# Row softmax in a graph layer: one exponential of 1024 columns in every step in place of one of 2048 in every second

## The chip, the cores and the metric

The kernel runs on one core of one Trainium2 chip. The metric is the device time of one execution in microseconds (us). A core has TensorE (PE, matrix products; weight loads are listed apart as PEld), VectorE (DVE), ScalarE (ACT), GpSimd (POOL) and SyncE (SP), each with its own instruction stream; they meet only through semaphores.

## The reference

4096 rows `x` attend to 4096 neighbours under a 0/1 matrix `adj`:

```python
h = relu(layernorm(x))
neib_att = tanh(neigh @ Wn1 + bn1) @ Wn2 + bn2        # 4096 x 32
value    = neigh @ Wv + bv                            # 4096 x 128
x_att    = tanh(h @ Wx1 + bx1) @ Wx2 + bx2            # 4096 x 32
ws = leaky_relu(x_att @ neib_att.T, 0.01)             # 4096 x 4096
ws = softmax(where(adj > 0, ws, NEG_BIG), axis=1)
out = x + concatenate([h @ Wfx + bfx, ws @ value], axis=1)
```

All inputs and the output are float32, `adj` is int32. The softmax is over all 4096 neighbours of a row.

## The kernel before, in words

**Tiles.** A tile is 128 rows of `x` by all 4096 neighbours; it is cut into 4 chunks of 1024 columns (`CHUNK`, `CHUNKS`). One chunk is a step `s`; 32 tiles make 128 steps. Four tiles make a round of 16 steps (`GSTEPS`), for which new rows of `x` are normalised, turned and projected as side work. Two tiles make a group `g` of 8 steps, whose weights are multiplied with `value` together.

**A chunk's way.** In step `s`:
- VectorE makes the bf16 mask of `adj` (`mask_of`, L679), two steps ahead.
- TensorE makes scores in the PSUM tile `ps` (`score`, L913 and L914). `ps` has two buffers, so the scores of step `s` wait on `leaked` of step `s - 2`. From step 11 on the mask of the upper 512 columns is not added here.
- ScalarE stores `Relu(99 * ps)` in `scores` (`rise`, L551).
- GpSimd adds the mask to the upper half of that (L455).
- VectorE, one step later, computes `(ps + scores) * 0.01`, which is the leaky relu, stores it in `scores`, and keeps the running maximum of the row in `top` (`leak`, L708). The reduction over a chunk starts from the entry of the chunk before, so the four leaks of a tile form a chain. After the fourth, `negate` (L719) writes `neg_top`, the bias of the exponential.
- ScalarE, five steps after the scores (`EXP_LAG`), takes the exponential in place with its row sums (`power`, L563). It does so for two chunks at once, in every second step: exponentials of 128 x 2048 in odd steps, none in even ones. An exponential with row sums is two records in the trace, an ACTIVATE and an ACTIVATION_READ_ACCUMULATOR.
- TensorE, eleven steps after the scores (`BACK_LAG`), turns 128 x 128 blocks of the exponentials into the PSUM tile `pt` (`turn`, L936), in two turns a step. Each turn is split into two float32r parts: `pt_hi` by ScalarE (`hi`, L525), `pt_lo` by VectorE (`lo`, L690). TensorE multiplies both with `value` in three products (`product`, L957 to L959), two turns behind. A turn waits on the `pt_lo` of two turns before, because `pt` has two buffers.
- When a group is through, ScalarE copies the product to `agg` (`aggregate`, L533), TensorE turns it back (L968), and VectorE scales it with the reciprocal of the row sums and adds it to `x` (L764).

**Order.** There is no scheduler. Each engine's stream is written out by its function `step(s)`:

```python
# ScalarE                         # VectorE                        # TensorE
hi(s, 0)                          leak(s)      # chunk s - 1       score(s, 0); score(s, 1)
aggregate(s)                      lo(s, 0)                         turn(s, 0)
rise(s)                           negate(s)                        product(s, -2)
hi(s, 1)                          close(s); neigh_rest(s)          turn(s, 1)
side(s)                           x_work(s)                        side(s)
power(s)                          lo(s, 1)                         product(s, -1)
                                  mask_of(s + 2)                   agg_turn(s)
```

Of the kernel before, what the change touches and what calls it, by code (L numbers as in the profile page):

```python
# [25 lines left out]
FP32 = mybir.dt.float32  # L26
# [3 lines left out]
ALU = mybir.AluOpType  # L30
ACT = mybir.ActivationFunctionType
AX = mybir.AxisListType

P = 128
# [7 lines left out]
CHUNK = 2 * BANK  # L42
CHUNKS = N_NEIGH // CHUNK
STEPS = GROUPS * TILES * CHUNKS
# [10 lines left out]
SLOPE = 0.01  # L55
# [10 lines left out]
TURN_X = 4  # L66
FILL = (6, 6, 6, 4, 0, 0, 0, 0)
EXP_LAG = CHUNKS + 1
HALF = 2 * CHUNK
HALVES = N_NEIGH // HALF  # L70
BACK_LAG = ASTEPS + 3
COPY_LAG = BACK_LAG + ASTEPS + 1
# [28 lines left out]
def build(nc, x, adj, neigh_t, small_of, wide_of, value_of, out):  # L101
    with ExitStack() as ctx:
        def sb(name, shape, dt):
            return ctx.enter_context(nc.sbuf_tensor(name, shape, dt))

        def sem(name):
            return ctx.enter_context(nc.semaphore(name))
# [16 lines left out]
        wide_x = sb("wide_x", [P, WIDE], FP32)  # L124
        ident = sb("ident", [P, P], FP32)
        ident_bf16 = ident.bitcast(BF16)[:, 1:2 * P:2]
        top = sb("top", [P, 2, CHUNKS], FP32)
        neg_top = sb("neg_top", [P, 2, 1], FP32)
        sums = sb("sums", [P, 2, TILES, HALVES], FP32)
        row_sum = sb("row_sum", [P, AT], FP32)  # L130
        inv_sum = sb("inv_sum", [P, 2, AT], FP32)
# [37 lines left out]
        ps = ctx.enter_context(nc.psum_tensor("ps_scores", [P, 2, CHUNK], FP32))  # L169
# [34 lines left out]
        risen = sem("risen")  # L204
        masked = sem("masked")
        leaked = sem("leaked")
        top_done = sem("top_done")
        exp_done = sem("exp_done")
        block_turned = sem("block_turned")
        hi_done, lo_done = sem("hi_done"), sem("lo_done")  # L210
# [66 lines left out]
        def chunk_of(s):  # L277

            return s // GSTEPS % 2, s // CHUNKS % TILES, s % CHUNKS
# [187 lines left out]
        def _(act):  # L467
# [85 lines left out]

            def power(s):
                e = s - EXP_LAG
                if 0 <= e < STEPS and e % 2 == 0:
                    parity, tile, c = chunk_of(e)
                    if c == 0:
                        act.wait_ge(top_done, e // CHUNKS + 1)
                        if tile == 0 and e >= 2 * GSTEPS:  # L560
                            act.wait_ge(sums_done, (e // GSTEPS - 1) * TILES // AT)
                    cols = scores[:, parity * TILES + tile, c * CHUNK:c * CHUNK + HALF]
                    act.activation(cols, cols, ACT.Exp, bias=neg_top[:, tile % 2, :],  # L563
                                   accum_out=sums[:, parity, tile, c // 2:c // 2 + 1]).then_inc(exp_done, 1)

            def side(s):
                if s == 0:
# [11 lines left out]
            def step(s):  # L579
                hi(s, 0)  # L580
                aggregate(s)
                rise(s)
                hi(s, 1)
                side(s)
                power(s)
# [5 lines left out]
        def _(dve):  # L591
# [74 lines left out]
            def mask_of(n):  # L666

                k = n
                if ADJ_RING <= n < ADJ_RING + FRONT:
                    source = adj_front[:, n - ADJ_RING, :]  # L670
                    dve.wait_ge(front_ready[(n - ADJ_RING) // LOAD], 16)
                else:
                    source = adj_in[:, n % ADJ_RING, :]
                    dve.wait_ge(adj_ready[n % ADJ_RING // LOAD], 16 * ((n - FRONT if n >= ADJ_RING else n) // ADJ_RING + 1))
                if n >= MASK_RING:
                    dve.wait_ge(scored, n - MASK_RING + 1)
                if n - MASK_RING >= POOL_MASKS:
                    dve.wait_ge(masked, n - MASK_RING + 1 - POOL_MASKS)
                dve.tensor_scalar(mask[:, n % MASK_RING, :], source, 0.0, MASKED, ALU.is_le,  # L679
                                  ALU.mult).then_inc(mask_done, 1)  # L680

            def lo(s, u):
                b = s - BACK_LAG
                if not 0 <= b < STEPS:
                    return
                j = 2 * b + u
                dve.wait_ge(hi_done, j + 1)
                if 2 * b + u >= 2:
                    dve.wait_ge(block_used, j - 1)
                dve.tensor_tensor(pt_lo[:, u], pt[:, u], pt_hi[:, (2 * b + u) % HI_RING].bitcast(FP32),  # L690
                                  ALU.subtract).then_inc(lo_done, 1)

            def leak(s):
                n = s - 1
                if not 0 <= n < STEPS:
                    return
                parity, tile, c = chunk_of(n)
                cols = scores[:, parity * TILES + tile, c * CHUNK:(c + 1) * CHUNK]
                dve.wait_ge(risen, n + 1)
                if n >= POOL_MASKS:  # L700
                    dve.wait_ge(masked, n + 1 - POOL_MASKS)
                if c:
                    dve.wait_ge(leaked, n)
                start = top[:, tile % 2, c - 1:c] if c else -3.0e38
                if c == 0 and n >= 2 * CHUNKS:
                    dve.wait_ge(top_done, n // CHUNKS - 1)
                dve.sem_inc(joined, 1)
                dve.tensor_tensor_reduce(cols, ps[:, n % 2], cols, SLOPE, start, ALU.add, ALU.max,  # L708
                                         top[:, tile % 2, c:c + 1]).then_inc(leaked, 1)

            def negate(s):
                n = s - 1
                if not 0 <= n < STEPS or n % CHUNKS != CHUNKS - 1:
                    return
                dve.wait_ge(leaked, n + 1)
                if n >= 2 * CHUNKS:

                    dve.wait_ge(exp_done, (n // CHUNKS - 1) * HALVES)
                dve.tensor_scalar(neg_top[:, n // CHUNKS % 2, :], top[:, n // CHUNKS % 2, CHUNKS - 1:CHUNKS],  # L719
                                  -1.0, None, ALU.mult).then_inc(top_done, 1)  # L720

            def neigh_rest(s):
                if value_due(s - 2) is not None:
                    value_low(value_due(s - 2))
                if s == 1:
                    att_low(1, NEIGH_GROUPS - 1)

            def x_work(s):
                if s == AHEAD_STATS:
                    for i in range(TILES):  # L730
                        x_stats(1, i)
                    x_aggr(1)
                for i in range(TILES):
                    if (e := x_due(s, X_STATS[i])) > 1:
                        x_stats(e, i)
                if (e := x_due(s, X_AGGR)) > 1:
                    x_aggr(e)
                if e := x_due(s, X_STACK[1]):
                    x_stack_low(e, e % 2, x_bank_late(e))
                if s == LEFT_0:  # L740
                    x_left_out(0, pa[:, 0, :])
                if e := x_due(s, X_LEFT):
                    x_left_out(e, x_bank_late(e))

            def close(s):
                b = s - SUM_LAG
                if b >= 0 and b % ASTEPS == 0 and b // ASTEPS < AGROUPS:
                    g = b // ASTEPS
                    first = g % (TILES // AT) * AT
                    dve.wait_ge(exp_done, (g + 1) * AT * HALVES)  # L750
                    wait(dve, sums_done, g)
                    dve.reduce_sum(row_sum[:, :], sums[:, g // (TILES // AT) % 2, first:first + AT],
                                   axis=AX.X).then_inc(row_sum_done, 1)
                    dve.wait_ge(row_sum_done, g + 1)
                    wait(dve, right_done, g - 1)
                    dve.reciprocal(inv_sum[:, g % 2, :], row_sum[:, :]).then_inc(sums_done, 1)
                b = s - FIN_LAG
                if b >= 0 and b % ASTEPS < AT and b // ASTEPS < AGROUPS:
                    g, i = b // ASTEPS, b % ASTEPS
                    if i == 0:  # L760
                        dve.wait_ge(agg_turned, g + 1)
                        dve.wait_ge(sums_done, g + 1)
                        dve.wait_ge(right_summed, g + 1)
                    last = dve.scalar_tensor_tensor(  # L764
                        right_of(g)[:, i, :], product_of(g)[:, i * P:(i + 1) * P], inv_sum[:, g % 2, i:i + 1],
                        right_of(g)[:, i, :], ALU.mult, ALU.add)
                    if i == AT - 1:
                        last.then_inc(right_done, 1)

            def step(s):  # L770
                if s < POOL_MASKS:
                    mask_of(s + 2)
                leak(s)
                lo(s, 0)
                negate(s)
                close(s)
                neigh_rest(s)
                x_work(s)
                lo(s, 1)
                if POOL_MASKS <= s < STEPS - 2:  # L780
                    mask_of(s + 2)
# [261 lines left out]
```

## Time and profile before

| | us |
|---|---|
| median of 3 runs | 489.14 (488.77 to 489.36) |
| the profiled execution | 488.76 |
| its span in the trace | 486.8 |
| TensorE busy | 467.1 |
| VectorE busy | 426.0 |
| ScalarE busy | 410.8 |
| GpSimd busy | 258.5 |

The first 31 us are the preparation of the neighbours, steps 0 to 10 fill the pipeline, steps 11 to 127 run all stages beside each other, and from 453 us on only turns and products are left. A group of instructions is shown by line, engine, operation, output and inputs. The busy time of TensorE holds overlapping pipelined products, so a high share says that it is the engine to watch, not that no time is lost on it; the waits say more. A step's place is found by counting: the n-th Relu of L551 is step n, the n-th pair of L525 copies is step 11 + n.

### The profile page before, as it was taken

What the parts mean: (1) busy time and instruction counts of PE and PEld (TensorE: products, weight loads), DVE (VectorE), ACT (ScalarE), POOL (GpSimd) and SP (SyncE); (2) the same over time, 40 slices, a digit from 0 to 9 for tenths busy, and PEclk for the clock granted to TensorE, in tenths of its full rate; (3) what the DMA queues carried; (4) which work ended last, traced back from release to release, by engine and by line L of the source; (5) the groups of instructions that cost most, each with busy time, mean ns of one, the idle gap of its engine ahead of it and who ended that gap; (6) DMA issues with size and microseconds to landing.
All of it is one profiled execution on the core that took longest, in us unless ns stands there. A gap on an engine that the chain in (4) does not pass through costs nothing.

```text
span 486.8 us, 10746 instructions
## 1 busy us (share of the span) xinstructions
PE 467.1 (96%) x3728; PEld 423.8 (87%) x3728; DVE 426.0 (88%) x852; ACT 410.8 (84%) x586; POOL 258.5 (53%) x361
## 2 busy tenths in 40 slices
PE   7987889999999999999999999999999999999897
PEld 7975679998899989998998989998999989988896
DVE  4678999989989999999999998989999888989654
ACT  2455898899988999899898998899889998999763
POOL 3108147844686457745685458745694555453200
PEclk9999999999999999999999999999999999999999
DMA  8944635557456754566445854476546465551000
GB/s 316 284 91 88 151 66 88 99 93 158 86 88 110 143 104 83 107 123 136 82 95 87 173 100 73 93 140 120 104 78 130 82 110 85 102 95 37 10 12 13
DMA packets 32373, 51.51 MB, mean 106 GB/s; under 512 B 2368, under 2 KB 22976, under 8 KB 32320
## 3 DMA queue, kind: packets, MB, share of 16 engines
q0 software_dynamic: 9216, 33.56, 42.1%
q1 hardware_dynamic: 22816, 17.17, 11.0%
q8 instruction: 30, 0.49, 0.4%
q10 hardware_dynamic: 288, 0.10, 0.1%
q14 instruction: 23, 0.19, 0.1%
HBM read 80.19 MB, written 4.19 MB: 173 GB/s over the span
## 4 chain that ended last, share of the span: by engine, by line
PE 74%; ACT 5%; issue 4%; DVE 4%; POOL 2%; DVEq 0%; ACTq 0%; POOLq 0%
PE ps_turned L936 20%; PE ps_product L957 11%; PE ps_product L959 11%; PE ps_product L958 11%; PE ps_scores L914 10%; PE ps_scores L913 6%; PE ps_product L879 3%; POOL scores L455 2%; ACT scores L551 2%; DVE pt_lo L690 2%; ACT scores L563 1%; PE ps_product L855 1%; ACT pt_hi L525 1%; PE ps_product L871 1%; DVE mask L679 1%
## 5 line engine op out<-in xcount | busy, mean ns | idle before, releaser
L690 DVE TENSOR_TENSOR pt_lo<-ps_turned,pt_hi 128x512 fp32r<-128x512 f32 x256 | 173.5, 686 | 35.3 <-ACT pt_hi L525 23.9
L455 POOL TENSOR_TENSOR scores<-scores,mask 128x512 f32<-128x512 f32 x117 | 136.2, 1164 | 118.6 <-ACT scores L551 118.4
L525 ACT ACTIVATE pt_hi<-ps_turned 128x512 fp32r<-128x512 f32 x256 | 155.4, 607 | 42.6 <-PE ps_turned L936 41.6
L957 PE MATMUL ps_product<-pt_hi,v_hi 128*128 128x256 f32 x512 | 165.0, 322 | 0.1
L936 PE MATMUL ps_turned<-ident,scores 128*128 128x128 f32 x1024 | 154.5, 273 | 2.0 <-DVE pt_lo L690 1.7
L959 PE MATMUL ps_product<-pt_lo,v_hi 128*128 128x256 f32 x512 | 144.3, 282 | 0.0
L958 PE MATMUL ps_product<-pt_hi,v_lo 128*128 128x256 f32 x512 | 144.0, 281 | 0.0
L551 ACT ACTIVATE scores<-ps_scores 128x1024 f32<-128x1024 f32 x128 | 132.1, 1032 | 10.3 <-PE ps_scores L914 10.3
L936 PEld LDWEIGHTS ps_turned<-ident,scores 128*128 128x128 f32 x1024 | 121.2, 140 | 21.6 <-DVE pt_lo L690 3.9
L563 ACT ACTIVATE scores<-scores,neg_top 128x2048 f32<-128x2048 f32 x64 | 129.1, 2018 | 0.0
L708 DVE CUSTOM_DVE_ANT_0 scores<-ps_scores,scores,top 128x1024 f32<-128x1024 f32 x96 | 122.5, 1276 | 1.1 <-ACT scores L551 0.9
L914 PE MATMUL ps_scores<-neib,xs 128*128 128x512 f32 x256 | 106.7, 496 | 0.0
L957 PEld LDWEIGHTS ps_product<-pt_hi,v_hi 128*128 128x128 f32 x512 | 97.3, 190 | 1.5 <-issue 1.2
L958 PEld LDWEIGHTS ps_product<-pt_hi,v_lo 128*128 128x128 f32 x512 | 97.3, 190 | 0.0
L959 PEld LDWEIGHTS ps_product<-pt_lo,v_hi 128*128 128x128 f32 x512 | 96.3, 188 | 0.0
L913 PE MATMUL ps_scores<-mask,ident 128*128 128x512 bf16 x139 | 53.6, 386 | 10.3 <-DVE top L708 6.3
L418 POOL DMA_DIRECT2D adj_in<-in_adj x60 | 35.4, 589 | 39.7 <-DVE mask L679 36.7
L679 DVE TENSOR_SCALAR mask<-adj_in 128x1024 bf16<-128x1024 bf16 x120 | 56.1, 469 | 0.1
L914 PEld LDWEIGHTS ps_scores<-neib,xs 128*128 128x128 f32 x256 | 49.5, 193 | 3.2
L708 DVE CUSTOM_DVE_ANT_0 scores<-ps_scores,scores 128x1024 f32<-128x1024 f32 x32 | 38.9, 1216 | 1.0 <-ACT scores L551 1.0
L913 PEld LDWEIGHTS ps_scores<-mask,ident 128*128 128x128 bf16 x139 | 13.4, 97 | 22.4 <-issue 17.3
L404 POOL TENSOR_SCALAR x_rows<-x_rows,mean_var,rstd 128x256 f32<-128x256 f32 x24 | 30.1, 1256 | 0.0
(71 smaller groups left out, 349.4 us busy)
## 6 DMA issues: line engine op xcount, KB each, us to landing
adj_in<-in_adj POOLq DMA_DIRECT2D x60, 512.0 KB, 5.5
scores<-in_neigh_t SPq DMA_DIRECT2D x8, 512.0 KB, 7.7
x_rows<-in_x SPq DMA_DIRECT2D x7, 512.0 KB, 5.7
x_left<-in_x SPq DMA_DIRECT2D x8, 256.0 KB, 5.7
x_right<-in_x SPq DMA_DIRECT2D x16, 128.0 KB, 5.2
scores<-in_adj POOLq DMA_DIRECT2D x4, 512.0 KB, 6.6
out_h<-x_left SPq DMA_DIRECT2D x8, 256.0 KB, 2.4
out_h<-x_right SPq DMA_DIRECT2D x16, 128.0 KB, 2.4
```

Of the source, the lines that this page charges most:

```text
L455: pool.tensor_tensor(half, half, mask[:, s % MASK_RING, BANK:CHUNK], ALU.add).then_inc(masked, 1)
L525: act.activation(pt_hi[:, (2 * b + u) % HI_RING], pt[:, u], ACT.Copy).then_inc(hi_done, 1)
L551: act.activation(scores[:, parity * TILES + tile, c * CHUNK:(c + 1) * CHUNK], ps[:, s % 2], ACT.Relu, scale=RISE).then_inc(risen, 1)
L563: act.activation(cols, cols, ACT.Exp, bias=neg_top[:, tile % 2, :], accum_out=sums[:, parity, tile, c // 2:c // 2 + 1]).then_inc(exp_done, 1)
L690: dve.tensor_tensor(pt_lo[:, u], pt[:, u], pt_hi[:, (2 * b + u) % HI_RING].bitcast(FP32), ALU.subtract).then_inc(lo_done, 1)
L708: dve.tensor_tensor_reduce(cols, ps[:, n % 2], cols, SLOPE, start, ALU.add, ALU.max, top[:, tile % 2, c:c + 1]).then_inc(leaked, 1)
L913: pe.matmul(ps[:, s % 2, half], ident_bf16, mask[:, s % MASK_RING, half], start=True, stop=False)
L914: last = pe.matmul(ps[:, s % 2, half], xs[:, parity, tile * P:(tile + 1) * P], neib[:, c * CHUNK + h * BANK:c * CHUNK + (h + 1) * BANK], s ...
L936: last = pe.transpose(pt[:, u, (k * AT + i) * P:(k * AT + i + 1) * P], scores[:, (g * AT + i) % (2 * TILES), (n * SPAN + k) * P:(n * SPAN ...
L957: pe.matmul(product_of(g), v_hi[:, block, :], high, start=block == 0, stop=False)
L958: pe.matmul(product_of(g), v_lo[:, block, :], high, start=False, stop=False)
L959: last = pe.matmul(product_of(g), v_hi[:, block, :], low, start=False, stop=block == BLOCKS - 1)
```

## The change

The exponential handles one chunk (`HALF = CHUNK`), in every step, with one entry of row sums for each chunk. The scores are stored negated (slope -0.01), with the running minimum in `low_top`; the exponential has scale -1 and takes the last entry of `low_top` as its bias directly. `negate`, `neg_top` and the semaphore `top_done` are gone. The exponential of a tile's first chunk waits on `leaked` instead. The leak of a tile's first chunk, which overwrites an entry pair of `low_top`, waits on `exp_done` of all chunks of two tiles before.

```diff
-HALF = 2 * CHUNK
+HALF = CHUNK
@@ ScalarE
             def power(s):
                 e = s - EXP_LAG
-                if 0 <= e < STEPS and e % 2 == 0:
+                if 0 <= e < STEPS:
                     parity, tile, c = chunk_of(e)
                     if c == 0:
-                        act.wait_ge(top_done, e // CHUNKS + 1)
+                        act.wait_ge(leaked, (e // CHUNKS + 1) * CHUNKS)
                         if tile == 0 and e >= 2 * GSTEPS:
                             act.wait_ge(sums_done, (e // GSTEPS - 1) * TILES // AT)
                     cols = scores[:, parity * TILES + tile, c * CHUNK:c * CHUNK + HALF]
-                    act.activation(cols, cols, ACT.Exp, bias=neg_top[:, tile % 2, :],
-                                   accum_out=sums[:, parity, tile, c // 2:c // 2 + 1]).then_inc(exp_done, 1)
+                    act.activation(cols, cols, ACT.Exp, bias=low_top[:, tile % 2, CHUNKS - 1:CHUNKS], scale=-1.0,
+                                   accum_out=sums[:, parity, tile, c:c + 1]).then_inc(exp_done, 1)
@@ VectorE
-                start = top[:, tile % 2, c - 1:c] if c else -3.0e38
+                start = low_top[:, tile % 2, c - 1:c] if c else 3.0e38
                 if c == 0 and n >= 2 * CHUNKS:
-                    dve.wait_ge(top_done, n // CHUNKS - 1)
+                    dve.wait_ge(exp_done, (n // CHUNKS - 1) * HALVES)
                 dve.sem_inc(joined, 1)
-                dve.tensor_tensor_reduce(cols, ps[:, n % 2], cols, SLOPE, start, ALU.add, ALU.max,
-                                         top[:, tile % 2, c:c + 1]).then_inc(leaked, 1)
-
-            def negate(s):
...
+                dve.tensor_tensor_reduce(cols, ps[:, n % 2], cols, -SLOPE, start, ALU.add, ALU.min,
+                                         low_top[:, tile % 2, c:c + 1]).then_inc(leaked, 1)
@@ VectorE, step(s)
                 leak(s)
                 lo(s, 0)
-                negate(s)
                 close(s)
```

The order on ScalarE before, in steps 23 to 25 (a round's steps 7 to 9), from the second copy of step 23; L563 is the exponential, L525 the `pt_hi` copy, L551 the Relu, L502 a copy of side work:

```order
L525 ACTIVATE pt_hi<-ps_turned 128x512 [waits block_used,block_turned]
L563 ACTIVATE scores,sums<-scores,neg_top 128x2048 [waits top_done]
L525 ACTIVATE pt_hi<-ps_turned 128x512 [waits block_used,block_turned]
L551 ACTIVATE scores<-ps_scores 128x1024 [waits scored]
L525 ACTIVATE pt_hi<-ps_turned 128x512 [waits block_used,block_turned]
L502 ACTIVATE x_rows_t<-ps_product 128x512 [waits x_wide,x_turned]
L525 ACTIVATE pt_hi<-ps_turned 128x512 [waits block_used,block_turned]
L551 ACTIVATE scores<-ps_scores 128x1024 [waits scored]
L525 ACTIVATE pt_hi<-ps_turned 128x512 [waits block_used,block_turned]
L563 ACTIVATE scores,sums<-scores,neg_top 128x2048
```

The same place of ScalarE in the changed kernel, where L561 is the exponential, L523 the `pt_hi` copy, L549 the Relu and L500 the copy of side work:

```order
L523 ACTIVATE pt_hi<-ps_turned 128x512 [waits block_used,block_turned]
L561 ACTIVATE scores,sums<-scores,low_top 128x1024 [waits leaked]
L523 ACTIVATE pt_hi<-ps_turned 128x512 [waits block_used,block_turned]
L549 ACTIVATE scores<-ps_scores 128x1024 [waits scored]
L523 ACTIVATE pt_hi<-ps_turned 128x512 [waits block_used,block_turned]
L500 ACTIVATE x_rows_t<-ps_product 128x512 [waits x_wide,x_turned]
L561 ACTIVATE scores,sums<-scores,low_top 128x1024
L523 ACTIVATE pt_hi<-ps_turned 128x512 [waits block_used,block_turned]
L549 ACTIVATE scores<-ps_scores 128x1024 [waits scored]
L523 ACTIVATE pt_hi<-ps_turned 128x512 [waits block_used,block_turned]
L561 ACTIVATE scores,sums<-scores,low_top 128x1024
```

Between two Relus of this stretch there is now exactly one exponential, where every second gap had none.

The order on VectorE before, around the first leak of a tile (the second L708 pair; the first is the fourth leak of the tile before), L690 being `pt_lo`:

```order
L708 ISA scores,top<-ps_scores,scores,top 128x1024 [waits leaked,risen,masked]
L708 ISA top 128x1
L690 TENSOR_TENSOR pt_lo<-ps_turned,pt_hi 128x512 [waits block_used,hi_done]
L719 TENSOR_SCALAR neg_top<-top 128x1 [waits exp_done,leaked]
L690 TENSOR_TENSOR pt_lo<-ps_turned,pt_hi 128x512 [waits block_used,hi_done]
L679 TENSOR_SCALAR mask<-adj_in 128x1024 [waits masked,scored,adj_ready1]
L708 ISA scores,top<-ps_scores,scores 128x1024 [waits top_done,risen,masked]
```

And in the changed kernel:

```order
L706 ISA scores,low_top<-ps_scores,scores,low_top 128x1024 [waits leaked,risen,masked]
L706 ISA low_top 128x1
L688 TENSOR_TENSOR pt_lo<-ps_turned,pt_hi 128x512 [waits block_used,hi_done] x2
L677 TENSOR_SCALAR mask<-adj_in 128x1024 [waits masked,scored,adj_ready1]
L706 ISA scores,low_top<-ps_scores,scores 128x1024 [waits exp_done,risen,masked]
```

The instruction between the two `pt_lo` is gone, and the wait on `exp_done` has moved from it to the first leak of the next tile. The orders of TensorE, GpSimd and SyncE hold the same instructions as before.

## Rows read from the trace of the kernel before

**Rows 1.** The page's busy times: us, share of the span, instructions.

```profile
PE 467.1 (96%) x3728; PEld 423.8 (87%) x3728; DVE 426.0 (88%) x852; ACT 410.8 (84%) x586; POOL 258.5 (53%) x361
```

**Rows 2.** Busy time of each engine in steps 64 to 79, then clock, DMA.

```profile
239.00:293.07 54.07, 53.60 (x422) 49.11 (x420) 50.61 (x103) 49.32 (x71) 34.32 (x47) 1.00 0.59 108
```

**Rows 3.** Waits, 77.37 to 401.16 us: who for whom: total, times, longest.

```profile
PEld ps_scores L913 <- issue: 5.2, 16, 0.4
...
PE ps_scores L913 <- DVE top L708: 2.0, 10, 0.2
PEld ps_turned L936 <- DVE pt_lo L690: 1.5, 6, 0.3
...
PEld ps_product L968 <- ACT agg L533: 1.1, 6, 0.2
```

**Rows 4.** Waits, 401.16 to 453 us.

```profile
PEld ps_scores L913 <- issue: 0.9, 2, 0.4
```

**Rows 5.** TensorE in order of time, steps 72 to 74: start, us, instruction.

```profile
266.18 0.60 PE L936 MATMUL ps_turned<-ident,scores 128*128 128x128 f32 x4
...
268.93 0.39 PE L913 MATMUL ps_scores<-mask,ident 128*128 128x512 bf16 x1
...
269.62 0.60 PE L936 MATMUL ps_turned<-ident,scores 128*128 128x128 f32 x4
...
271.93 0.39 PE L913 MATMUL ps_scores<-mask,ident 128*128 128x512 bf16 x1
```

**Rows 6.** ScalarE in order of time, steps 71 to 73.

```profile
265.53 2.02 ACT L563 ACTIVATE scores<-scores,neg_top 128x2048 f32<-128x2048 f32 x1
267.43 0.21 ACT L563 ACTIVATION_READ_ACCUMULATOR scores<-scores,neg_top 128x1 f32 x1
267.51 0.60 ACT L525 ACTIVATE pt_hi<-ps_turned 128x512 fp32r<-128x512 f32 x1
267.99 1.04 ACT L551 ACTIVATE scores<-ps_scores 128x1024 f32<-128x1024 f32 x1
268.90 0.62 ACT L525 ACTIVATE pt_hi<-ps_turned 128x512 fp32r<-128x512 f32 x1
269.37 0.64 ACT L502 ACTIVATE x_rows_t<-ps_product 128x512 f32<-128x512 f32 x1
270.26 0.60 ACT L525 ACTIVATE pt_hi<-ps_turned 128x512 fp32r<-128x512 f32 x1 [0.25 <-PE ps_turned L936]
```

**Rows 7.** VectorE in order of time: leaks of steps 72 and 73, `pt_lo` before.

```profile
269.55 0.69 DVE L690 TENSOR_TENSOR pt_lo<-ps_turned,pt_hi 128x512 fp32r<-128x512 f32 x1 [0.65 <-ACT pt_hi L525]
...
270.49 1.22 DVE L708 CUSTOM_DVE_ANT_0 scores<-ps_scores,scores 128x1024 f32<-128x1024 f32 x1
...
273.23 1.28 DVE L708 CUSTOM_DVE_ANT_0 scores<-ps_scores,scores,top 128x1024 f32<-128x1024 f32 x1
```

**Rows 8.** ScalarE's groups by shape: busy us, mean ns, idle before.

```profile
L525 ACT ACTIVATE pt_hi<-ps_turned 128x512 fp32r<-128x512 f32 x256 | 155.4, 607 | 42.6 <-PE ps_turned L936 41.6
L551 ACT ACTIVATE scores<-ps_scores 128x1024 f32<-128x1024 f32 x128 | 132.1, 1032 | 10.3 <-PE ps_scores L914 10.3
L563 ACT ACTIVATE scores<-scores,neg_top 128x2048 f32<-128x2048 f32 x64 | 129.1, 2018 | 0.0
L563 ACT ACTIVATION_READ_ACCUMULATOR scores<-scores,neg_top 128x1 f32 x64 | 13.2, 207 | 0.0
...
L506 ACT ACTIVATE agg<-ps_product,small_x 128x128 f32<-128x128 f32 x8 | 3.2, 402 | 0.0
```

**Rows 9.** The tail in order of time, steps 131 and 132.

```profile
461.43 0.63 PE L936 MATMUL ps_turned<-ident,scores 128*128 128x128 f32 x4 [0.96 <-DVE pt_lo L690]
...
463.74 2.00 ACT L563 ACTIVATE scores<-scores,neg_top 128x2048 f32<-128x2048 f32 x1
```

**Rows 10.** ScalarE in order of time, steps 9 and 10.

```profile
58.57 2.04 ACT L563 ACTIVATE scores<-scores,neg_top 128x2048 f32<-128x2048 f32 x1
...
60.55 1.06 ACT L551 ACTIVATE scores<-ps_scores 128x1024 f32<-128x1024 f32 x1
```

More of the change, by code:

```diff
@@ L126, in build @@
         ident_bf16 = ident.bitcast(BF16)[:, 1:2 * P:2]
-        top = sb("top", [P, 2, CHUNKS], FP32)
-        neg_top = sb("neg_top", [P, 2, 1], FP32)
+        low_top = sb("low_top", [P, 2, CHUNKS], FP32)
         sums = sb("sums", [P, 2, TILES, HALVES], FP32)
@@ L206, in build @@
         leaked = sem("leaked")
-        top_done = sem("top_done")
         exp_done = sem("exp_done")
@@ L703, in leak @@
                     dve.wait_ge(leaked, n)
-                start = top[:, tile % 2, c - 1:c] if c else -3.0e38
+                start = low_top[:, tile % 2, c - 1:c] if c else 3.0e38
                 if c == 0 and n >= 2 * CHUNKS:
-                    dve.wait_ge(top_done, n // CHUNKS - 1)
+                    dve.wait_ge(exp_done, (n // CHUNKS - 1) * HALVES)
                 dve.sem_inc(joined, 1)
-                dve.tensor_tensor_reduce(cols, ps[:, n % 2], cols, SLOPE, start, ALU.add, ALU.max,
-                                         top[:, tile % 2, c:c + 1]).then_inc(leaked, 1)
-            def negate(s):
[L712 to L720, printed above, removed]
+                dve.tensor_tensor_reduce(cols, ps[:, n % 2], cols, -SLOPE, start, ALU.add, ALU.min,
+                                         low_top[:, tile % 2, c:c + 1]).then_inc(leaked, 1)
             def neigh_rest(s):
```

## Prediction

> **What bounds the kernel now.** I read the busy shares first: TensorE 467.1 of 486.8 us, VectorE 426.0, ScalarE 410.8 [rows 1]. Three engines lie within 14%, so a share alone does not name the bound. The granted clock is 1.00 in the busy row of a full 16-step round, 239.00 to 293.07 us; there TensorE is busy 53.60 of 54.07 us, VectorE 50.61, ScalarE 49.32 [rows 2]. So the clock plays no part, TensorE is nearly the bound, and what can be won is the small idle time that is left on it.
>
> The waits say what that idle time is. From step 16 (77.37) to step 112 (401.16) TensorE waits 5.2 + 2.0 us before a step's score products, 1.5 us before a turn for the low halves `pt_lo`, and 1.1 us for the `agg` copy: 9.8 us in six rounds [rows 3]. In the sixteen steps after that it is 0.9 us before scores [rows 4]. The wait before scores is for `leaked` of two steps ago, since `ps` has two buffers.
>
> The reason stands in the order of time. Steps 72 and 73 of TensorE start their turns at 266.18 and 269.62 [rows 5]. ScalarE runs a 2048-column exponential in the odd step 71 (265.53, readout 267.43), and only then comes to the first `pt_hi` copy of step 72 at 267.51, which is 1.33 us after the turn started. In step 73 no exponential precedes, and the copy starts at 270.26, 0.64 us after its turn, having waited 0.25 us for TensorE [rows 6]. Every later hand-over inherits this: the Relu of step 72 starts at 267.99 (1.81 after the turn), then comes GpSimd's mask addition, and VectorE's leak of step 72 starts at 270.49, or 4.31 us after the turn of that step. For step 73 the leak comes at 273.23, 3.61 after the turn [rows 7]. The even steps are thus about 0.7 us late, and it is their leak that releases the scores two steps later.
>
> **What the change removes.** The 32 `negate` instructions go from VectorE: 426.0 us is not its bound, each lies in a place where VectorE waits 0.65 us for ScalarE's next `pt_hi` [rows 7], so I count them at nothing. Negative scale and slope, and the minimum for the maximum, use the same two instructions on tiles of the same size: nothing, with no row that says otherwise. If the leak were dearer by 0.1 us in the negated form, VectorE would still have 1.6 us less work than a round lasts (50.61 + 1.6 against 54.07), so it would be covered.
>
> **What it adds: 64 exponentials and 64 readouts.** ScalarE has 512 columns in 607 ns and 1024 in 1032 ns, so 0.83 ns per column and a fixed 0.18 us; a 128-column tanh with a bias tile takes 402 ns, so about 0.30 us fixed. The exponential of 2048 takes 2018, of which 1.70 are columns: 0.32 us fixed [rows 8]. One of 1024 should take 0.85 + 0.32 = 1.17 us. In order of time an instruction hands over before its end: 1.90 us from exponential to readout, 0.08 from readout to the next copy [rows 6]. So one of 1024 occupies 1.17 - 0.12 + 0.08 = 1.13 us, two occupy 2.26 where one of 2048 occupied 1.98. That is +0.28 us a pair, 17.9 us of ScalarE time in the kernel. The bounds: below, half of the old one each (0.99, no cost at all); above, the full 1.17 plus the full 207 ns of a readout (1.37, +0.76 a pair). I take 1.13, since it is made of the nearest rows.
>
> Is there room? A round gets 8 extra pairs' cost, 8 x 0.28 = 2.2 us: ScalarE goes from 49.32 to 51.6 of 54.07 [rows 2]. It fits, and stays below TensorE's 53.60. Without side work a ScalarE step becomes 0.48 + 0.90 + 0.48 + 1.13 = 2.99 us (the first three from the starts in [rows 6]), and TensorE's step without side work lasts 3.00 (268.93 to 271.93 [rows 5]). The engines match within a row's accuracy: a copy that starts 0.64 after its turn starts so again a step later. ScalarE loses ground only in steps with side work of its own, about 0.3 to 0.5 us, and TensorE nearly always has side work in the same or the next steps.
>
> The Trainium skill, "ScalarE: Activation LUTs", section "What ACT_TABLE_LOAD costs", speaks against the change: an ACTIVATE whose bias is a per-partition operand costs some 280 ns beside its columns whatever its size, and neighbours overlap by some 93 ns, so cutting one in two buys nothing and costs a fixed part. For the old exponential it gives 1986 ns, and the trace agrees with 2018 [rows 8]. By it the addition would be an estimated 12 us of ScalarE for the 64 more, without a price for the readouts, against my 17.9; if ScalarE were the bound, either would be lost time.
>
> **What it moves.** ScalarE now meets an exponential in every step, after the step's second copy, where before it met two steps' worth in odd steps. The copy of even steps should begin 0.64 instead of 1.33 after its turn, and Relu, mask addition and leak move forward with it, from 4.31 to about 3.61. That leak ends near 3.61 + 1.22 = 4.83 after the turn of its step; the scores that need it follow at least 2 x 3.00 - 0.69 = 5.31 after (0.69: 268.93 to 269.62 [rows 5]). TensorE then does not wait for it. The last chunk of a row is exponentiated one step later than before; its block turns come three and more steps after that, and so I count nothing.
>
> **The new wait.** The leak of each row's first chunk now waits until ScalarE has finished the exponentials of two rows before, the last of which stands at the end of the step before. On time, ScalarE reaches its end at 0.64 + 1.86 + 1.13 = 3.63 after the turn, with the semaphore about 3.7. The leak itself would start at 3.61: 0.1 us later in each of 30 rows, within the 0.48 us of slack just found (5.31 against 4.83). Where ScalarE has a `x_rows_t` copy ahead of that exponential (step 8 of a round) it is some 0.5 later still; the transposes put 0.44 us more on TensorE there too (step 72 lasts 3.44 [rows 5]). So 0.1 us each over 7 rounds, 0.7 us in all. Behind this leak on VectorE stand both `pt_lo` of the step and the next mask; their readers are a step later on TensorE, with over half a microsecond in hand.
>
> **The sum.** Of the 9.8 us in the six rounds I take two thirds, 6.5; the rest belongs to GpSimd's normalisation, to side work and to places that have no exponential ahead of them. The 0.9 us in steps 112 to 127 I take whole, since less side work stands there. In the tail, TensorE stands 0.96 us at 461.43 behind an exponential, and the one at 463.74 (2.00 us) delays copies and `agg` again [rows 9]: 1.5 together, since a 1.13 us exponential fits a 2.3 us tail step. In the opening the exponential at 58.57 holds the Relu of step 10 until 60.55 [rows 10]; one that occupies 1.13 us in place of 1.98 gives 0.85, say 0.9. Together 6.5 + 0.9 + 1.5 + 0.9 = 9.8, less 0.7 for the new wait and 1.0 for lateness through ScalarE's side work: 8.1 us. The profiled execution took 488.76 us, so 480.7. The median of the runs is 489.14, 0.4 more, of which I add a small part: 480.8 us.
>
> **Rivals.**
> A, most of the gain is not there (TensorE's idle time has other causes, or the next thing is late by as much: `pt_lo`, the mask, GpSimd). For it speaks that only 0.47 us of a 54.07 us round is idle on TensorE [rows 2]; against it, that the busy time contains short waits between pipelined products, and the waits listed are 1.6 us a round. Then a quarter to a third of 9.8 remains: about 486.
> B, nothing measurable: gain and new wait cancel, 488.8. It needs 0.3 us at each of the 30 first chunks.
> C, slower: ScalarE becomes the bound. Place: every step, through the fixed part of the exponential and its readout. At 1.37 us each a round has 49.32 + 8 x 0.76 = 55.4 us of ScalarE work, 1.3 more than it lasts now; over 7 rounds +9, less 2.4 kept in opening and tail: 495. It decides from an occupancy at which 16 exponentials cost 54.07 - 49.32 = 4.75 us more than 8 old ones: (8 x 1.98 + 4.75) / 16 = 1.29 us each. Against it stand the overlaps seen in [rows 6]. The late first leak would add to it, since both come from the same lateness.
> D, the change does not even the steps out: ScalarE's order would have to keep two exponentials together. The order has one in each step, so I give this no chance of its own.
>
> **How the numbers follow.** Forecast 0.60, within 477.5 to 484: the low end takes the waits whole (9.8 + 0.9 + 1.5 + 0.9, less 1.7, is 11.4), the high end half of them (6.5 less 1.7 is 4.8). A 0.18, B 0.08, C 0.14. What can be told from no change here is 0.2%, about 1 us. Faster has the forecast and A, and a little of B: 0.79; same 0.08; slower 0.13. The range reaches from 477 to 489.5, through A and B; most of C is left out.
>
> **What would show it.** The exponential of 1024 near 1.17 us and its occupancy near 1.13. The first copy of even and of odd steps both 0.6 to 0.9 us after the turn. A round of 52.9 to 53.4 us instead of 54.07. Waits before scores reduced to a third, while ScalarE is busy some 428 us (410.8 + 17.9). VectorE waiting at first chunks for ScalarE's exponential, 0.1 us at a time, would confirm the new wait; waits of 0.3 us and more there, passed on to TensorE's scores, would make the prediction wrong, as would ScalarE without idle time in a round.

## The result, and the profile after

| | us |
|---|---|
| before, median (4 runs) | 489.25 (488.77 to 489.43) |
| changed, median (4 runs) | 485.37 (484.90 to 485.68) |
| ratio | 0.9929, interval 0.9917 to 0.9941 |
| changed, the profiled execution | 485.15, span 482.8 |

The change makes the kernel 3.9 us faster, where 8.3 were forecast: the direction was right and the time lies inside the range, but the gain is under half of the forecast.

The page's busy times, beside [rows 1]:

```profile
PE 464.3 (96%) x3728; PEld 424.5 (88%) x3728; DVE 427.7 (89%) x820; ACT 428.3 (89%) x714; POOL 258.4 (54%) x361
```

ScalarE has 17.5 us more, as forecast (17.9). VectorE lost 32 instructions (4.6 us in the group of L719) and is busy 1.7 us longer all the same; that is the first hint of something that the prediction did not contain. It is the masks that grew, with their number and shape unchanged; the group in the kernel before, then in the changed one:

```profile
L679 DVE TENSOR_SCALAR mask<-adj_in 128x1024 bf16<-128x1024 bf16 x120 | 56.1, 469 | 0.1
```

```profile
L677 DVE TENSOR_SCALAR mask<-adj_in 128x1024 bf16<-128x1024 bf16 x120 | 61.1, 510 | 0.1
```

The groups of ScalarE, beside [rows 8]:

```profile
L561 ACT ACTIVATE scores<-scores,low_top 128x1024 f32<-128x1024 f32 x128 | 151.5, 1183 | 0.0
...
L561 ACT ACTIVATION_READ_ACCUMULATOR scores<-scores,low_top 128x1 f32 x128 | 29.5, 230 | 0.0
```

The same steps 71 to 73 of ScalarE in order of time (start, us, instruction), beside [rows 6]:

```profile
265.38 1.22 ACT L561 ACTIVATE scores<-scores,low_top 128x1024 f32<-128x1024 f32 x1
266.43 0.27 ACT L561 ACTIVATION_READ_ACCUMULATOR scores<-scores,low_top 128x1 f32 x1
266.52 0.66 ACT L523 ACTIVATE pt_hi<-ps_turned 128x512 fp32r<-128x512 f32 x1
266.99 1.10 ACT L549 ACTIVATE scores<-ps_scores 128x1024 f32<-128x1024 f32 x1
...
268.85 1.26 ACT L561 ACTIVATE scores<-scores,low_top 128x1024 f32<-128x1024 f32 x1
269.89 0.30 ACT L561 ACTIVATION_READ_ACCUMULATOR scores<-scores,low_top 128x1 f32 x1
269.98 0.70 ACT L523 ACTIVATE pt_hi<-ps_turned 128x512 fp32r<-128x512 f32 x1
```

TensorE's first turns of steps 72 and 73:

```profile
265.84 0.60 PE L922 MATMUL ps_turned<-ident,scores 128*128 128x128 f32 x4
...
269.27 0.60 PE L922 MATMUL ps_turned<-ident,scores 128*128 128x128 f32 x4
```

An exponential of 1024 columns occupies 265.38 to 266.52, 1.14 us; forecast 1.13. The copies come 0.68 and 0.71 us after their turns, where before it was 1.33 and 0.64. For ScalarE the steps are evened out. But the round of steps 64 to 79 shrank only from 54.07 [rows 2] to 53.82 us:

```profile
238.82:292.64 53.82, 53.20 (x422) 49.07 (x420) 51.04 (x99) 51.53 (x87) 33.92 (x47) 1.00 0.58 109
```

The columns are the length, then PE, PEld, DVE, ACT, POOL, clock, DMA. ScalarE rose to 51.53 (51.6 forecast), VectorE to 51.04 from 50.61. The waits from step 16 to 112 (77.85 to 399.68), beside [rows 3]:

```profile
PEld ps_scores L899 <- issue: 5.9, 18, 0.5
DVE scores L706 <- ACT scores L561: 5.6, 12, 0.6
...
PE ps_scores L899 <- DVE low_top L706: 1.7, 6, 0.3
...
PEld ps_turned L922 <- issue: 0.5, 3, 0.2
```

The wait for `agg` is gone, and TensorE's waits before turns fell from 1.5 us (for `pt_lo`) to 0.5, for which the trace names no cause; that is about the 2.0 us by which these six rounds became shorter (323.79 to 321.83). The waits before scores are 7.6 us where they were 7.2. They have moved to other steps. The second row is new: VectorE's leak waits for an exponential, the wait that the change added.

The opening, VectorE's leak of step 8 and then TensorE's scores of step 10:

```profile
57.97 1.23 DVE L706 CUSTOM_DVE_ANT_0 scores<-ps_scores,scores 128x1024 f32<-128x1024 f32 x1 [1.87 <-ACT scores L561]
```

```profile
59.35 0.38 PE L899 MATMUL ps_scores<-mask,ident 128*128 128x512 bf16 x1 [1.50 <-DVE low_top L706]
```

The leak of step 8, a first leak, waits 1.87 us for the exponential that ScalarE makes in step 8, and the scores of step 10 wait behind it. In the rounds the two places are the scores of a round's steps 10 and 14. VectorE, steps 73 and 77, the first leaks of two tiles, each with the mask before it:

```profile
268.84 0.69 DVE L688 TENSOR_TENSOR pt_lo<-ps_turned,pt_hi 128x512 fp32r<-128x512 f32 x1 [0.41 <-PE ps_product L945]
269.45 0.42 DVE L677 TENSOR_SCALAR mask<-adj_in 128x1024 bf16<-128x1024 bf16 x1
270.48 1.23 DVE L706 CUSTOM_DVE_ANT_0 scores<-ps_scores,scores 128x1024 f32<-128x1024 f32 x1 [0.61 <-ACT scores L561]
...
283.21 0.77 DVE L677 TENSOR_SCALAR mask<-adj_in 128x1024 bf16<-128x1024 bf16 x1
283.90 1.21 DVE L706 CUSTOM_DVE_ANT_0 scores<-ps_scores,scores 128x1024 f32<-128x1024 f32 x1
```

And GpSimd at the second place:

```profile
281.83 1.16 POOL L453 TENSOR_TENSOR scores<-scores,mask 128x512 f32<-128x512 f32 x1 [0.96 <-ACT scores L549]
282.97 0.73 POOL L363 TENSOR_TENSOR x_left<-x_left,wide_x 128x256 f32<-128x256 f32 x1
```

TensorE's last product and the scores behind it, at the first place (step 74) and at the second (step 78):

```profile
271.45 0.28 PE L945 MATMUL ps_product<-pt_lo,v_hi 128*128 128x256 f32 x1
271.86 0.38 PE L899 MATMUL ps_scores<-mask,ident 128*128 128x512 bf16 x1
...
284.68 0.28 PE L945 MATMUL ps_product<-pt_lo,v_hi 128*128 128x256 f32 x1
285.27 0.38 PE L899 MATMUL ps_scores<-mask,ident 128*128 128x512 bf16 x1 [0.31 <-DVE low_top L706]
```

The products follow each other at 0.12 us; what a start comes later than that is counted as late here. The first leak waits 0.61 us for ScalarE; the scores of step 74 then start at 271.86, 0.29 late. At the second place the leak shows no wait, but the mask ahead of it takes 0.77 us where 0.42 is its time: it starts at 283.21 while GpSimd adds to `x_left` until 283.70, and is done just under 0.3 us after that. Here the scores of step 78 are 0.47 us late. In the kernel before, the mask of this place came first and took its 0.42, and GpSimd's addition was the one that was longer, 0.91 in place of 0.73:

```profile
283.81 0.42 DVE L679 TENSOR_SCALAR mask<-adj_in 128x1024 bf16<-128x1024 bf16 x1
```

```profile
283.91 0.91 POOL L365 TENSOR_TENSOR x_left<-x_left,wide_x 128x256 f32<-128x256 f32 x1
```

The scores of this step were late in the kernel before as well. How late the scores start, by the same count, as the mean of the six rounds: a round's step 14 has 0.36 us before and 0.42 after, step 10 has 0.02 and 0.26, step 8 has 0.15 and nothing, and steps 5 and 6 together have 0.28 and 0.25. So the change took the lateness of step 8 away and added that of step 10, and in step 14 one cause took the place of another. This gave two theories beside the forecast's own: 1, the new wait; 2, the mask has moved forward into GpSimd's addition. As the third I took the longer ScalarE time itself.

### The profile page after: what moved, and what is told of

Read it like the earlier page. It is cut to its first block, busy times and chain, and to the rows that moved or that the text cites. A ratio compares the mean times of both kernels' runs of the same rounds, so it can differ in the third digit from the quotient of the medians.

```text
span 482.8 us, 10844 instructions
## 1 busy us (share of the span) xinstructions
PE 464.3 (96%) x3728; PEld 424.5 (88%) x3728; DVE 427.7 (89%) x820; ACT 428.3 (89%) x714; POOL 258.4 (54%) x361
## 4 chain that ended last, share of the span: by engine, by line
PE 75%; ACT 5%; issue 3%; DVE 3%; POOLq 0%; POOL 0%; DVEq 0%; ACTq 0%
PE ps_turned L922 20%; PE ps_product L943 11%; PE ps_product L945 11%; PE ps_product L944 11%; PE ps_scores L900 10%; PE ps_scores L899 6%; PE ps_product L865 3%; ACT scores L561 3%; ACT pt_hi L523 2%; DVE scores L706 2%; PE ps_product L857 1%; PE ps_product L841 1%; ACT scores L549 1%; PE ps_product L848 1%; PE ps_product L954 1%
## 5 line engine op out<-in xcount | busy, mean ns | idle before, releaser
L523 ACT ACTIVATE pt_hi<-ps_turned 128x512 fp32r<-128x512 f32 x256 | 158.1, 618 | 20.9 <-PE ps_turned L922 20.3
L561 ACT ACTIVATE scores<-scores,low_top 128x1024 f32<-128x1024 f32 x128 | 151.5, 1183 | 0.0
L549 ACT ACTIVATE scores<-ps_scores 128x1024 f32<-128x1024 f32 x128 | 133.3, 1041 | 9.6 <-PE ps_scores L900 9.4
L706 DVE CUSTOM_DVE_ANT_0 scores<-ps_scores,scores,low_top 128x1024 f32<-128x1024 f32 x96 | 122.5, 1276 | 0.9 <-ACT scores L549 0.4
L677 DVE TENSOR_SCALAR mask<-adj_in 128x1024 bf16<-128x1024 bf16 x120 | 61.1, 510 | 0.1
L402 POOL TENSOR_SCALAR x_rows<-x_rows,mean_var,rstd 128x256 f32<-128x256 f32 x24 | 31.6, 1319 | 0.0
```

The costliest lines, as they stand in the source:

```text
L523: act.activation(pt_hi[:, (2 * b + u) % HI_RING], pt[:, u], ACT.Copy).then_inc(hi_done, 1)
L549: act.activation(scores[:, parity * TILES + tile, c * CHUNK:(c + 1) * CHUNK], ps[:, s % 2], ACT.Relu, scale=RISE).then_inc(risen, 1)
L561: act.activation(cols, cols, ACT.Exp, bias=low_top[:, tile % 2, CHUNKS - 1:CHUNKS], scale=-1.0, accum_out=sums[:, parity, tile, c:c + 1]). ...
L706: dve.tensor_tensor_reduce(cols, ps[:, n % 2], cols, -SLOPE, start, ALU.add, ALU.min, low_top[:, tile % 2, c:c + 1]).then_inc(leaked, 1)
```

## The experiments

Each was timed in five rounds; ratios are to the kernel before on the same chip. The changed kernel's is 0.9929 [0.9917, 0.9941].

| | median us | ratio | interval |
|---|---|---|---|
| e1 wait moved to the fourth leak | 482.93 | 0.9878 | 0.9863 to 0.9893 |
| e2 split alone | 483.26 | 0.9886 | 0.9873 to 0.9900 |
| e3 negated form alone | 488.77 | 0.9998 | 0.9989 to 1.0007 |
| e4 `x_left` addition in step 14 | 483.57 | 0.9897 | 0.9884 to 0.9911 |
| e5 e1 and e4 | 481.19 | 0.9843 | 0.9829 to 0.9856 |
| e6 e5, second half in step 16 | 479.50 | 0.9807 | 0.9794 to 0.9821 |
| e7 exponentials one step earlier | 482.25 | 0.9869 | 0.9855 to 0.9882 |
| e8 e5 with two exponentials of 512 | 500.42 | 1.0238 | 1.0224 to 1.0251 |
| e9 before, addition in step 14 | 489.02 | 1.0006 | 0.9995 to 1.0016 |
| e10 before, steps 14 and 16 | 487.47 | 0.9970 | 0.9959 to 0.9981 |

**e1, the wait at the fourth leak.** Only the fourth entry of a tile's row in `low_top` is read as a bias, so only the fourth leak has to wait.

```diff
-                if c == 0 and n >= 2 * CHUNKS:
+                if c == CHUNKS - 1 and n >= 2 * CHUNKS:
                     dve.wait_ge(exp_done, (n // CHUNKS - 1) * HALVES)
```

> The changed kernel with the wait on the exponentials of two tiles before put at a tile's fourth leak in place of its first (only the fourth entry of low_top is read as a bias). Nothing else differs. Theory 1, the new wait ate the missing 4.5 us: the opening gets back 0.9 us, each of the round's stalls behind a first leak goes (0.3 to 0.5 us, 6 rounds, two a round), so 481.5 to 482.5 us against 485.4. Theory 2, the stalls come from masks that VectorE makes while GpSimd works, and the wait stands beside them: only the opening gains, 484.3 to 485. Theory 3, the longer ScalarE time as such: no difference, 485.4.

The ratio is 0.0051 lower, 2.5 us; at 482.93 us it lies 0.4 us above what theory 1 expected and below what the other two did. VectorE's first leaks of steps 8, 72 and 76, in its trace:

```profile
56.39 1.23 DVE L706 CUSTOM_DVE_ANT_0 scores<-ps_scores,scores 128x1024 f32<-128x1024 f32 x1 [0.27 <-ACT scores L549]
...
268.61 1.22 DVE L706 CUSTOM_DVE_ANT_0 scores<-ps_scores,scores 128x1024 f32<-128x1024 f32 x1
...
281.78 0.77 DVE L677 TENSOR_SCALAR mask<-adj_in 128x1024 bf16<-128x1024 bf16 x1
282.46 1.21 DVE L706 CUSTOM_DVE_ANT_0 scores<-ps_scores,scores 128x1024 f32<-128x1024 f32 x1
```

In the opening the leak comes after the Relu again (56.39 instead of 57.97), and the one of step 72 directly behind its mask. The opening up to the turn of step 16 lost 0.5 us, steps 16 to 112 lost 1.6 (321.83 to 320.21), the rest 0.2; the expectation had 0.9 for the opening. The mask before the first leak of step 76 is as long as it was. So theory 1 holds for its own places and leaves the other. Theory 3, which expected no difference, is out.

**e2 and e3, one half of the change each.** e2 keeps `top`, `neg_top` and `negate` and only splits (`neg_top` lies in an unused corner of `agg`); e3 keeps the 2048 columns and only negates.

```diff
 e2, against the kernel before
-HALF = 2 * CHUNK
+HALF = CHUNK
-                if 0 <= e < STEPS and e % 2 == 0:
+                if 0 <= e < STEPS:
-                                   accum_out=sums[:, parity, tile, c // 2:c // 2 + 1]
+                                   accum_out=sums[:, parity, tile, c:c + 1]
 e3, against the changed kernel: the same lines the other way
```

> The kernel before with exponentials of 1024 columns in every step, but the positive scores, the maximum and the negation on VectorE kept; so it has no wait of a first leak on ScalarE. Theory 1: 482 to 483 us (as e1, with the 32 negations covered). Theory 2: 484.5 to 485.5, as the changed kernel. Theory 3: the split alone gives 485.4 and the negated form nothing.

> The changed kernel with exponentials of 2048 columns in every second step: the negated form alone. The wait of a first leak is then on an exponential of an odd step before, long done. All theories: the negations were covered, so within 0.5 us of before, 488.7 to 489.5. If the negated form had a price or a gain of its own it would show here.

The whole gain is the split's. The negated form alone changes nothing that can be measured, so the 32 negations were covered, as the prediction had it. In company with the split it costs 2.1 us (0.9929 less 0.9886). In steps 16 to 112 that is the wait: e2 takes 320.24 us there, as e1 does. The opening of e2 is no such proof. Its leak of step 8 does not wait, and yet it has 46.95 us up to the turn of step 16, as much as the changed kernel, with the mask at 68.16 beside an addition of GpSimd:

```profile
68.16 1.00 DVE L679 TENSOR_SCALAR mask<-adj_in 128x1024 bf16<-128x1024 bf16 x1
```

```profile
68.15 0.72 POOL L365 TENSOR_TENSOR x_left<-x_left,wide_x 128x256 f32<-128x256 f32 x1
```

**e4, GpSimd's addition away from the mask.** In an even step it stands behind the adj load, which waits for the mask that it used to hold up.

```diff
-X_LEFT_LOAD, X_SUM = 8, (13, 18)
+X_LEFT_LOAD, X_SUM = 8, (14, 18)
```

> The changed kernel with the first half of GpSimd's x_left addition in step 14 of a round in place of 13, behind the adj load that waits on the mask; so it no longer runs while VectorE makes the mask of the following step 14. Theory 2: the mask at 283.21 takes 0.42 in place of 0.77 us, the stall of 0.47 before the scores of step 14 shrinks to 0.1 to 0.2, 6 x 0.3 = 1.8 us: 483.6. Theory 1: that leak would still wait on ScalarE's exponential, to about 283.45 in place of 283.90, so part of it comes too: 484 to 484.5. Theory 3: 485.4.

The ratio is 0.0032 lower, 1.6 us. VectorE and GpSimd at the same place:

```profile
282.77 0.42 DVE L677 TENSOR_SCALAR mask<-adj_in 128x1024 bf16<-128x1024 bf16 x1
283.17 1.23 DVE L706 CUSTOM_DVE_ANT_0 scores<-ps_scores,scores 128x1024 f32<-128x1024 f32 x1
```

```profile
281.37 1.16 POOL L453 TENSOR_TENSOR scores<-scores,mask 128x512 f32<-128x512 f32 x1 [0.93 <-ACT scores L549]
284.37 1.17 POOL L453 TENSOR_TENSOR scores<-scores,mask 128x512 f32<-128x512 f32 x1 [1.85 <-ACT scores L549]
286.65 0.57 POOL L416 DMA_DIRECT2D adj_in<-in_adj  x1 [1.10 <-DVE mask L677]
287.24 0.74 POOL L363 TENSOR_TENSOR x_left<-x_left,wide_x 128x256 f32<-128x256 f32 x1
```

The mask has its 0.42 us back once GpSimd is idle beside it, and the median, 483.57, is what theory 2 expected (483.6). Its profiled execution was the slowest of the four (484.38) and has only 0.9 us less in steps 16 to 112 than the changed kernel (320.92); e5 below, which differs from e1 by the same edit, has 1.8 less there (320.21 to 318.42). Both theories are right, each for a part.

**e5 and e6, both, and the next place.** e5 has both edits. e6 also takes the second half of the addition out of a round's step 2, where GpSimd is most crowded.

```diff
 e6, against e5
-X_LEFT_LOAD, X_SUM = 8, (14, 18)
+X_LEFT_LOAD, X_SUM = 8, (14, 16)
```

> The late wait of e1 and the moved x_left addition of e4 together. e1 stands 2.5 us and e4 1.6 us under the changed kernel by their ratios. If the two causes are separate places of a round, the sum: 4.1 under, 481.2 us. If both ratios hold the same stall (the one before the scores of step 14), no more than e1: 482.9.

> e5 with the second half of the x_left addition moved too, from step 18 (a round's step 2, where GpSimd also has a normalisation, the x_right addition and an adj load in one go) to step 16. The mask of step 2 then waits less (1.33 us now where 0.42 is its own time) and the stall before the scores of step 5 (0.25 in e1) goes: 0.25 x 6 = 1.5 us under e5, 479.7. If that mask's length is covered, as e5.

Both came out within 0.2 us of what was expected. The causes add up, 0.0051 + 0.0032 = 0.0083 against 0.0086 measured for e5. e6 beats both kernels, by 9.3 us (0.9807) and 5.9 us. Its round of steps 64 to 79:

```profile
235.83:288.67 52.84, 52.84 (x422) 49.14 (x421) 49.93 (x99) 51.32 (x87) 34.44 (x47) 1.00 0.60 111
```

TensorE is busy 52.84 of 52.84 us: the waits before scores are gone (from 77.9 to 399 us its trace lists none), and TensorE's own work is the bound.

**e7, the wait kept, its exponential earlier.**

```diff
-EXP_LAG = CHUNKS + 1
+EXP_LAG = CHUNKS
```

> The changed kernel, its wait at the first leak untouched, with exponentials four steps behind the scores in place of five (EXP_LAG). The last exponential of two tiles before then ends a whole step before the first leak asks for it, so the wait costs nothing without being moved. Theory 1 (the wait's price is 2.5 us): as e1, 482.5 to 483.3. If e1 gained by something else than this wait: 485.4.

482.25 us, 0.9869, no worse than e1: the price was the wait's, not something else that moving it had disturbed. It was a matter of one step's distance. That it is 0.4 us better still than e1 (0.0009 of ratio, within both intervals) is not explained.

**e8, where ScalarE becomes the bound.** e5 with two exponentials of 512 columns in a step; `sums`, with twice the entries, lies in an unused corner of `agg` here.

```diff
-                    cols = scores[:, parity * TILES + tile, c * CHUNK:c * CHUNK + HALF]
-                    act.activation(...)
+                    for k in range(2):
+                        cols = scores[:, parity * TILES + tile, c * CHUNK + k * BANK:c * CHUNK + (k + 1) * BANK]
+                        last = act.activation(cols, cols, ACT.Exp, ..., accum_out=sums[:, parity, tile, 2 * c + k:2 * c + k + 1])
+                    last.then_inc(exp_done, 1)
```

> e5 with every exponential cut again, two of 512 columns a step, each with its readout: asks where ScalarE becomes the bound. From the fixed part (1183 ns at 1024 columns, 0.83 ns each: 0.33 fixed, and 0.04 less by overlap and readout) two of 512 occupy 2 x 0.72 = 1.43 against 1.14 us: a ScalarE step 3.29 where TensorE's is 3.00. Theory C, ScalarE then bounds: a round 16 x 3.29 + 2.4 = 55.0 us, 1.8 more than e5's, and 12 to 14 us in all: 494. If ScalarE still had slack: under 484.

19.2 us over e5, where 12 to 14 were expected in all. Steps 16 to 112 alone have 13.8 us of it (318.42 to 332.20), and the round is 55.45 us where 55.0 were expected; steps 112 to 128, opening and tail have 2.8, 1.9 and 1.1 us more, which the expectation lacked. ScalarE in order of time in step 73 (272.38 to the next step's copy), then the round:

```profile
272.38 0.82 ACT L562 ACTIVATE scores<-scores,low_top 128x512 f32<-128x512 f32 x1
273.00 0.29 ACT L562 ACTIVATION_READ_ACCUMULATOR scores<-scores,low_top 128x1 f32 x1
273.09 0.81 ACT L562 ACTIVATE scores<-scores,low_top 128x512 f32<-128x512 f32 x1
273.70 0.29 ACT L562 ACTIVATION_READ_ACCUMULATOR scores<-scores,low_top 128x1 f32 x1
273.80 0.68 ACT L523 ACTIVATE pt_hi<-ps_turned 128x512 fp32r<-128x512 f32 x1
```

```profile
245.00:300.45 55.45, 54.34 (x422) 49.11 (x421) 50.77 (x99) 55.16 (x120) 34.87 (x47) 1.00 0.56 105
```

Two occupy 1.42 us, 0.28 more than one of 1024. The first split cost the same 0.28 us per pair and gained; the second has ScalarE busy 55.16 of 55.45 us and loses. Rival C was a true mechanism, one split away.

**e9 and e10, the same edits on the kernel before.** The edit of e4 and the two of e6, there.

> The kernel before with the first half of the x_left addition in step 14: was the collision of that addition with VectorE's mask there already? In the trace of before the mask of that place takes 0.42 us, its own time, because it comes 0.6 us later than in the changed kernel. If the collision came with the change: 488.5 to 489, no difference. If it was there before: 1.6 us less, 487.2.

> The kernel before with both halves moved (steps 14 and 16). The stall before the scores of a round's step 5 is in the trace of before as well (0.37 us), from the mask of step 2 that waits for GpSimd (0.90 us on average). If it is worth as much there as in e6: 6 x 0.35, about 2 us less than e9, 486.8. If the even steps' lateness takes its place: 488.5.

e9 is no different from before: the collision of step 13 was not there, so the change made it. e10 gains 1.4 us (2 were expected), so the crowded step 2 cost something already. The change lengthens the mask of that step too, from 0.90 to 1.33 us as the mean of the six rounds, but the scores that follow are no later for it (0.28 and 0.25 us in steps 5 and 6). The mask at 249.83 in the kernel before, and the same mask in e10:

```profile
249.83 1.01 DVE L679 TENSOR_SCALAR mask<-adj_in 128x1024 bf16<-128x1024 bf16 x1
```

```profile
249.27 0.42 DVE L679 TENSOR_SCALAR mask<-adj_in 128x1024 bf16<-128x1024 bf16 x1
```

## Why the prediction was too high, point by point

- **The exponential's size**: right. 1.14 us against 1.13, ScalarE 17.5 us more against 17.9.
- **What it moves**: right for ScalarE, not for VectorE. As the mean of the six rounds the first copy of even steps starts 0.64 us after its turn in place of 1.18, and the Relu 1.20 in place of 1.72. The leak of even steps, forecast at 3.61 in place of 4.31, starts 4.46 after its turn in place of 4.54. It comes forward in a round's step 6 (4.44 to 3.95) and goes back where the new wait is (step 8: 4.34 to 4.62). e5, with both causes gone, has 3.95 at step 8 and 4.29 as the mean. The forecast was read off one pair of steps; what holds the other leaks where they are no run here isolates.
- **The negations at nothing**: right, by e3.
- **The tail and steps 112 to 127**: the sixteen steps gained 1.5 us (turn of step 112 to that of 128: 51.29 to 49.76), forecast 0.9; the end of the turns came 1.0 us sooner after that, forecast 1.5. Together 2.6 against 2.4, by two errors that cancel.
- **The new wait, 0.7 us**: this is the first step that failed; e1 and e7 show 2.5 and 2.9 us. The prediction priced it in a step without side work, found 0.1 us and held that covered, and counted 0.1 a round for the step that has a copy ahead of the exponential. In that step the leak's wait is as forecast (0.61 us against 0.1 and 0.5), but TensorE's scores are 0.29 late, because the slack was 0.3 us and not the 0.92 counted (0.48 and the 0.44 of the transposes). The transposes delay the product that the `pt_lo` ahead of the leak waits for (0.41 us at 268.84), so the leak could start only when its mask was done at 269.87, which is 4.03 us after its turn and not 3.61; and the scores start 1.38 us after the leak does, not 1.22. The prediction's own sign of being wrong, waits of 0.3 us and more that reach the scores, came true. And the opening was left out of this term: there the wait is 1.87 us, on the path. The opening's +0.9 became a loss of 0.3 (46.67 to 46.95 us from the first scores to the turn of step 16), and of e1's 2.5 us it has 0.5.
- **The sum's two thirds of the waits, 6.5 us**: the second step that failed. It took the work that comes forward as free of what it meets there. The mask came forward into GpSimd's addition and cost 1.6 us (e4, e9). The sum names GpSimd only as something that keeps a part of the old waits, not as a new one; rival A does name the mask and GpSimd as what may be late next. With its 1.0 for lateness through side work the term is 5.5 us; the six rounds gained 2.0 (323.79 to 321.83), 3.6 with the wait moved (e1) and 5.4 with both edits (e5).
- **Together**: with both gone, e5 stands 7.7 us under before, beside the 8.8 that the forecast is without its 0.7 for the wait. That it comes so near is in part luck: the opening and the tail were put 0.7 and 0.5 us too high, steps 112 to 127 0.85 too low (51.29 to 49.54 in e5, where 0.9 was forecast). In the changed kernel two terms of cost were missing or too small, by 1.8 and 1.6 us. Of the 1.1 us left between 8.1 and the profiled executions' 3.6, 0.7 is the opening, which gained only 0.2 us even without the wait (46.44 us in e1) where 0.9 was counted.
- **The rivals**: A, a gain of which most is not there, comes nearest (486 us), by the next thing being late, which it names. C is refuted for this change and shown for the next split.

Of the lengthened mask the Trainium skill has the rule, "SBUF — State Buffer", section "Who interferes with whom": VectorE in one of its two-port modes and GpSimd share a pair of ports, and whoever comes first keeps it for a whole instruction. The traces agree in who is longer: GpSimd's addition came first at 282.97 and the mask took 0.77 us, the mask came first in the kernel before and the addition took 0.91; apart from each other they take 0.42 (e4) and 0.74. They agree only roughly in the length: the mask is done 0.28 us after the addition ends, not its whole 0.42. That it is this port and not another shared thing no run here shows.

## What to carry to other kernels

When a stage is made earlier, look up what every instruction that comes forward with it will run beside, on the engines that have nothing to do with the change: the gain may be spent there. Price a new wait in the step with the most side work and in the pipeline's filling, not in the plain step, and put it at the last instruction that needs it: here three steps later, at no cost. Cutting an instruction in two pays as long as the engine has room within a round (here 2.2 us of 4.8), and the same cut again costs 19 us.

## What the runs showed that was not expected

- The mask of a round's crowded step 2 is stretched to 1.44 us from 0.42 (changed kernel, at 303.06, with GpSimd's mask addition running from 303.05 for 1.16 us). It ends 0.29 us after that addition, as the mask at 283.21 ends 0.28 us and that of e2 at 68.16 ends 0.29 us after theirs.

```profile
303.06 1.44 DVE L677 TENSOR_SCALAR mask<-adj_in 128x1024 bf16<-128x1024 bf16 x1
```

- ScalarE's readout record grew from 207 to 230 ns, and a `pt_hi` copy from 607 to 618, while starts stayed as far apart as before (0.47 us from a copy to the Relu where it was 0.48, 0.09 from a readout to the next copy where it was 0.08). A longer record next to a busier neighbour was not a dearer instruction here; starts are the better measure of what an engine spends.
